# A graph-attention kernel: scores turned by transposes, or computed a second time already turned

## The reference, cut to what matters

```python
h = jnp.maximum(_layernorm(x, axis=-1), 0.0)
# layer 1: attention over the graph's neighbours
qkv = h @ W_qkv + b_qkv                       # 8 heads, 16 features each
scores = einsum('bhqd,bhkd->bhqk', q, k) / 4
attn = softmax(where(adj, scores, -inf), axis=-1)
x = x + einsum('bhqk,bhkd->bhqd', attn, v) @ W_out + b_out
h = jnp.maximum(_layernorm(x, axis=-1), 0.0)
# layer 2: causal, row-normalised similarities
A_l = zero_diag(max(cos(h @ Wl, h @ Wl), 0));  A_g = zero_diag(exp(-dist2(h @ Wg) / 2))
K = 0.9 * rows_normalised(A_l * adj) + 0.1 * rows_normalised(A_g * adj)
x = x + (K @ (h @ Wv)) @ Wo
```

## Time and profile before

| | us |
|---|---|
| median of 3 runs | 953.59 (953.18 to 954.37) |
| span of the profiled execution (first to last instruction) | 952.0 |
| PE busy | 869.2 (91%) |
| DVE busy | 800.4 (84%) |
| ACT busy | 686.6 (72%) |
| POOL busy | 189.4 (20%) |
| mean granted TensorE clock | 0.993 |

### The profile page before, as it was taken

The page is one execution under the profiler, slowest core; times in us unless marked ns, Lnnn a source line. Parts: engine busy times, 40 slices in busy tenths (PEclk is TensorE's granted clock), DMA queues, the critical chain, the costliest instruction groups (busy, mean ns, idle before and its releaser), DMA issues.

```text
span 952.0 us, 21653 instructions
## 1 busy us (share of the span) xinstructions
PE 869.2 (91%) x6067; PEld 612.4 (64%) x6067; DVE 800.4 (84%) x2460; ACT 686.6 (72%) x1185; POOL 189.4 (20%) x270
## 2 busy tenths in 40 slices
PE   2688999999999999999999999999999999999977
PEld 1454658576685857667585766758576675858565
DVE  2777889798988989898898989899898989979765
ACT  1387877787877777787777778777877878787721
POOL 1221222131212213121221312122131221211110
PEclk9899999999999999999999999999999999999999
DMA  2321212121111212111111211111121111110000
GB/s 66 94 78 51 62 34 67 57 67 33 56 55 33 66 55 66 33 55 55 36 63 55 66 36 52 55 42 59 54 66 39 50 55 51 62 35 1 12 12 12
DMA packets 62423, 47.56 MB, mean 50 GB/s; under 512 B 7600, under 2 KB 62384, under 8 KB 62384
## 3 DMA queue, kind: packets, MB, share of 16 engines
q1 hardware_dynamic: 62384, 47.09, 16.3%
HBM read 30.28 MB, written 16.78 MB: 49 GB/s over the span
## 4 chain that ended last, share of the span: by engine, by line
PE 74%; DVE 6%; issue 5%; ACT 4%; DVEq 0%; POOL 0%; ACTq 0%; POOLq 0%
PE turn L545 18%; PE pv L557 13%; PE adj L572 12%; PE adj L566 11%; PE score L535 11%; PE work L579 5%; ACT probs L919 2%; PE work L566 2%; PE work L657 2%; PE work L642 1%; DVE bn_sb L729 1%; DVE resid L861 1%; DVE masked L764 1%; ACT probs_t L912 1%; ACT col_term L964 1%
## 5 line engine op out<-in xcount | busy, mean ns | idle before, releaser
L919 ACT ACTIVATE probs<-masked,neg_max 128x512 f32<-128x512 f32 x512 | 368.6, 727 | 154.6 <-DVE neg_max L764 149.1
L764 DVE CUSTOM_DVE_ANT_0 masked<-score,mask_add 128x512 f32<-128x512 f32 x512 | 344.2, 685 | 35.3 <-PE score L535 33.8
L545 PE MATMUL turn<-ident,probs 128*128 128x128 f32 x2048 | 311.5, 274 | 3.5 <-ACT probs_t L912 2.0
L545 PEld LDWEIGHTS turn<-ident,probs 128*128 128x128 f32 x2048 | 253.4, 141 | 53.2 <-issue 9.7
L912 ACT COPY probs_t<-turn 128x512 f32<-128x512 f32 x384 | 222.4, 579 | 23.6 <-PE turn L545 23.1
L535 PE MATMUL score<-qk_rows 96*128 96x512 bf16 x512 | 198.4, 388 | 12.0 <-DVE neg_max L764 11.0
L557 PE MATMUL pv<-probs_t,v_cols 128*32 128x512 f32 x1024 | 135.7, 604 | 0.4 <-issue 0.4
L535 PEld LDWEIGHTS score<-qk_rows 96*128 96x128 bf16 x512 | 49.9, 98 | 109.5 <-DVE neg_max L764 59.1
L772 DVE COPY probs_t<-turn 128x512 f32<-128x512 f32 x128 | 87.8, 686 | 0.0
L572 PE MATMUL adj<-z,adj_cos 128*128 128x130 f32 x512 | 67.8, 276 | 1.5 <-DVE adj_cos L780 0.8
L572 PE MATMUL adj<-z,adj_rbf 128*128 128x130 f32 x512 | 67.3, 275 | 0.0
(11 more groups left out here) (101 smaller groups left out, 1025.2 us busy)
## 6 DMA issues: line engine op xcount, KB each, us to landing
qk_rows<-split_dram SPq DMA_DIRECT2D x384, 64.0 KB, 2.3
split_dram<-split SPq DMA_DIRECT2D x32, 384.0 KB, 2.6
x_sb<-in_x_dram SPq DMA_DIRECT2D x16, 256.0 KB, 2.9
out_dram<-out_sb SPq DMA_DIRECT2D x16, 256.0 KB, 2.3
masked<-in_adj_dram SPq DMA_DIRECT2D x1, 256.0 KB, 3.4
wqkv_sb<-in_L_gnn_W_qkv_dram SPq DMA_DIRECT2D x1, 192.0 KB, 2.6
bias_v<-in_L_gnn_b_qkv_dram SPq DMA_DIRECT2D x1, 64.0 KB, 3.1
bias_out<-in_L_gnn_b_out_dram SPq DMA_DIRECT2D x1, 64.0 KB, 3.8
```

Source lines behind the costliest of these rows:

```text
L545: last = pe.transpose(turn_bank[u % 2][:, j * P:(j + 1) * P], probs[:, u % 4, j * P:(j + 1) * P], ident[:, :])
L764: dve.tensor_tensor_reduce(masked[:, u % 4, :], score_bank[u % 2][:, :], mask_add[:, u % T, :], -SCALE, 3.0e38, ALU.add, ALU.min, neg_max[ ...
L919: act.activation(probs[:, u % 4, :], masked[:, u % 4, :], ACT.Exp, bias=neg_max[:, u:u + 1], scale=-1.0).then_inc(probs_ready.sem, 1)
```

## The change

What it does:

- The scaled probabilities are no longer turned. Instead each tile's scores are computed a second time with the operands changed round (k stationary, q moving), so that the keys come out on the partitions. The 96 contraction rows get three more on the q side, the negated row maxima of the queries as three bf16 parts, against rows of ones on the k side: the maxima are subtracted by the contraction.
- The mask is added to every turned tile by one more bf16 matmul into the same bank, identity times `bar_t` (0 or -2^100, turned).
- ACT takes exp straight from PSUM, with a scale and no bias, into `probs_t`. The copies by ACT and DVE (L912, L772) and the tiles `probs` and `turn_bank` are gone.
- DVE's pass over the first scores now only serves the maxima; its tile goes to `scrap`. After every 16 tiles DVE splits 16 columns of maxima into three bf16 parts (four small instructions), PE turns them, ACT copies them, and SP writes them as three contraction rows into `qk_rows` (three DMAs per half batch).
- The turned scores run 21 slots behind the scores (`LAG`) instead of 3.
- `qk_rows` is doubled, so that the next batch's rows are loaded without waiting for this batch's scores; `x_resid` has 4 buffers, `x1` 2, `v_cols` 3, and the moves by POOL (L455, L471, L483) are gone.
- The loop is gone: every engine runs over one list of slots from -32 to 583, each piece of work has a slot relative to its batch (`due`), and the pieces have new places in `AT`. The mask's setup moves ahead of the first v product; POOL's constants come first, with a memset of rows of ones in `qk_rows`.

The diff, cut to its core:

```diff
-TURN_LAG = 3
-VECTOR_UNITS = (3, 5, 6, 17, 21, 22, 27, 28)
+SLOTS = 32
+LAG = 21
 AT = {
...
+    "ln_moments": (-32,), "ln_scale": (-30,), "hT": (-29,), "hT_split": (-28,), "ln_rstd": (-27,),
+    "q": (-26,), "k": (-24,), "qk_store": (-22,), "rows0": (-18,), "x_biased": (-16,), "x_next": (-14,),
+    "v": (-12,), "rows1": (-11,),
+    "max_split": (16, 32), "max_turn": (17, 33),
+    "pv": (28, 32, 36, 40, 44, 48, 52, 56), "pv_copy": (41, 57), "y": (44, 59), "yT": (60,), "attn": (62,),
+    "ln2_moments": (63,), "ln2_rstd": (63,), "ln2_scale": (66,), "h2T": (68,), "z": (70, 71, 72, 73),
+    "z_sums": (74,), "zgT": (74,), "zgT_read": (75,), "z_norms": (76,), "col": (78,), "zlT": (79,),
+    "rbf": (81, 83, 89, 93), "rbf_exp": (82, 84, 90, 93), "rbf_mask": (84, 86, 92, 95),
+    "cos": (82, 89, 92, 94), "mix_cos": (95, 96, 100, 102), "mix_rbf": (96, 98, 100, 102), "store": (103,),
 }
+FIRST, LAST = -32, 104
...
+    def due(slot, name):
+        for nth, at in enumerate(AT[name]):
+            batch, rest = divmod(slot - at, SLOTS)
+            if rest == 0 and 0 <= batch < B:
+                return batch, nth
+        return None
...
+        qk_rows = sb("qk_rows", [P, 2, 2, H, N], BF16)
+        v_cols = sb("v_cols", [P, 3, T, H, 32])
...
SP, for s in slots:
+                if hit := due(s, "max_turn"):
+                    b, g = hit
+                    reached(sp, max_copied, b, g + 1)
...
+                    for part in range(3):
+                        sp.dma_start(
+                            qk_rows[ROWS + part:ROWS + part + 1, b % 2, 0, g * HG:(g + 1) * HG, :],
+                            max_rows[part * HALF:(part + 1) * HALF, g, :]).then_inc(max_loaded[g].sem, 16)
...
POOL, setup:
+            pool.memset(v_cols[:, :, :, :, DH + 1:32], 0.0)
+            pool.memset(v_cols[:, :, :, :, DH:DH + 1], 1.0).then_inc(s_columns.sem, 1)
+            pool.wait_ge(s_columns.sem, 1)
+            pool.memset(qk_rows[ROWS:P, :, 1, :, :], 1.0).then_inc(s_consts.sem, 1)
...
PE:
-            def turn(batch, u):
-                reached(pe, probs_ready, batch, u + 1)
...
-                for j in range(T):
-                    last = pe.transpose(turn_bank[u % 2][:, j * P:(j + 1) * P],
-                                        probs[:, u % 4, j * P:(j + 1) * P], ident[:, :])
-                last.then_inc(turned.sem, 1)
+            def turned_scores(b, w):
+                g, k = divmod(w, HALF)
+                j, hl = divmod(k, HG)
+                h = g * HG + hl
+                if k == 0:
+                    reached(pe, max_loaded[g], b)
+                reached(pe, probs_ready, b, w - 1)
+                pe.matmul(turned_bank[w % 2][:, :], ident_b[:, :], bar_t[:, j, :], start=True, stop=False)
+                pe.matmul(turned_bank[w % 2][:, :], qk_rows[0:ROWS + 3, b % 2, 1, h, j * P:(j + 1) * P],
+                          qk_rows[0:ROWS + 3, b % 2, 0, h, :], start=False,
+                          stop=True).then_inc(turned_filled.sem, 1)
...
+                if hit := due(s, "max_turn"):
+                    b, g = hit
+                    reached(pe, max_lo, b, g + 1)
+                    work_bank_free(pe, b, "max_turn", g)
+                    pe.transpose(work_bank[0:3 * HALF, 0:P // 2].bitcast(BF16),
+                                 max_parts[:, g, :, :].rearrange("p c u -> p (c u)"),
+                                 ident_b[:, :]).then_inc(max_turned.sem, 1)
...
DVE:
-                        dve.tensor_tensor_reduce(masked[:, u % 4, :], score_bank[u % 2][:, :],
-                                                 mask_add[:, u % T, :], -SCALE, 3.0e38, ALU.add, ALU.min,
-                                                 neg_max[:, u:u + 1]).then_inc(masked_ready.sem, 1)
...
-                        dve.tensor_copy(probs_t[:, h // HG, h % HG, :, t * P:(t + 1) * P],
-                                        turn_bank[u % 2][:, :].rearrange("p (j q) -> p j q", j=T)
-                                        ).then_inc(copied_vector.sem, 1)
+                    dve.tensor_tensor_reduce(scrap[:, u % 2, :], score_bank[u % 2][:, :], mask_add[:, u % T, :], -1.0,
+                                             3.0e38, ALU.add, ALU.min,
+                                             neg_max[:, u // HALF, u % HALF:u % HALF + 1]
+                                             ).then_inc(max_ready.sem, 1)
+                if hit := due(s, "max_split"):
...
+                    dve.tensor_copy(max_parts[:, g, 0, :], neg_max[:, g, :]).then_inc(max_hi.sem, 1)
+                    reached(dve, max_hi, b, g + 1)
+                    dve.tensor_tensor(max_rest[:, :], neg_max[:, g, :], max_parts[:, g, 0, :],
+                                      ALU.subtract).then_inc(max_rest_ready.sem, 1)
+                    reached(dve, max_rest_ready, b, g + 1)
+                    dve.tensor_copy(max_parts[:, g, 1, :], max_rest[:, :]).then_inc(max_mid.sem, 1)
+                    reached(dve, max_mid, b, g + 1)
+                    dve.tensor_tensor(max_parts[:, g, 2, :], max_rest[:, :], max_parts[:, g, 1, :],
+                                      ALU.subtract).then_inc(max_lo.sem, 1)
...
ACT:
-                        act.activation(probs[:, u % 4, :], masked[:, u % 4, :], ACT.Exp,
-                                       bias=neg_max[:, u:u + 1], scale=-1.0).then_inc(probs_ready.sem, 1)
...
+                if hit := tile_due(s, LAG):
+                    b, w = hit
+                    k = w // HG
+                    reached(act, turned_filled, b, w + 1)
+                    if w % HG == 0:
+                        reached(act, pv_filled, b, k - 3)
+                    act.activation(probs_t[:, k % 4, w % HG, :], turned_bank[w % 2][:, :], ACT.Exp,
+                                   scale=SCALE).then_inc(probs_ready.sem, 1)
+                if hit := due(s, "max_turn"):
+                    b, g = hit
+                    reached(act, max_turned, b, g + 1)
+                    reached(act, max_loaded[g], b - 1)
+                    act.copy(max_rows[:, g, :], work_bank[0:3 * HALF, 0:P // 2].bitcast(BF16)
+                             ).then_inc(max_copied.sem, 1)
```

More of the change, by code:

```diff
@@ L79, in graph_blocks, with tile_due @@
     HG = H // GROUPS
-    SLOTS = H * T
     ROWS = len(Q_PARTS) * DH
-    HALF = H // 2
+    HALF = SLOTS // GROUPS
+    SETS = GROUPS * T
     SCALE = float(DH) ** -0.5
     ZC = 3 * D + 2
-    assert D == P and T == 4 and HG * 32 == P
-    copied_by_vector = [u for u in range(SLOTS) if u in VECTOR_UNITS]
-    copied_by_scalar = [u for u in range(SLOTS) if u not in VECTOR_UNITS]
+    assert D == P and T == 4 and HG * 32 == P and SLOTS == H * T
+    def due(slot, name):
[4 more added lines that the diff above has]
+        return None
+    def tile_due(slot, lag):
+        batch, u = divmod(slot - lag, SLOTS)
+        return (batch, u) if 0 <= batch < B else None
+    slots = range(FIRST, LAST + SLOTS * (B - 1))
     with ExitStack() as ctx:
@@ L324, in work_bank_free @@
-        def work_bank_free(engine, i, use):
-            at = [name for name, _, _, _ in WORK_USES].index(use)
-            for back in range(1, len(WORK_USES) + 1):
-                _, sig, nth, offset = WORK_USES[(at - back) % len(WORK_USES)]
-                batch = i + offset - (1 if back > at else 0)
-                if isinstance(batch, int) and not 0 <= batch < B:
-                    continue
-                reached(engine, sig, batch, nth)
-                return
+        WORK_TURNS = sorted(
+            (AT[name][nth] + SLOTS * b, order, name, nth, b)
+            for b in range(B)
+            for order, (name, nth) in enumerate((
+                ("max_turn", 0), ("max_turn", 1), ("hT", 0), ("q", 0), ("k", 0), ("v", 0), ("y", 0), ("y", 1),
+                ("yT", 0), ("attn", 0), ("h2T", 0), ("zgT", 0), ("col", 0), ("zlT", 0))))
@@ L428, in body @@
[L428 to L445 removed]
+            pool.wait_ge(s_ident.sem, 1)
@@ L518, in rest_of_setup @@
                           stop=True).then_inc(s_wvo.sem, 1)
[L519 to L524 removed]
+                pe.wait_ge(s_ident_b.sem, 1)
                 pe.wait_ge(s_consts.sem, 1)
```

973 lines of the change are left out of this document (474 added, 499 removed).

## The result

The changed kernel takes 990.87 us (median of 4 runs, 983.95 to 998.25), the kernel before in the same comparison 953.38: ratio 1.039, 95% interval 1.034 to 1.044. It is slower by 3.9%. The forecast was 944 us, faster than before; the measured time lies above its range (918 to 962). The profiled execution took 983.95 us with a span of 981.9. The runs differ by up to 14 us among themselves; their mean granted clock was 0.989 in the fastest and 0.955 in the slowest. The kernel before has no such spread (953.0 to 954.4).

The account below looks back on a forecast made before the run. TensorE's work was taken as the bound, 55.1 us a steady period against 55.4. Span 36.5 + 33.7 + 36.5 + 46.9 + 661.2 + 49.7 + 36.0 + 42.1 = 942.6, so 944 us, range 918 to 962.

Parts of the forecast that it names:

- steps 1, 2, 3, 5: Tile stays 0.66 us; exp 0.60, ACT some 26 us a period; DVE 46.1; maxima's DMAs hidden in steady state, margin 1.4.
- rival C: Maxima's DMAs land late in every period, costing 1 us each: 956 us in all; chance 0.08.
- Rival D: Streamed bf16 matmuls cost less than 0.22 us, so DVE binds at 48 us a period: 846 us; chance 0.01.
- step 4: New order: a 10.7 us DVE chain from attn to hT's turning makes PE wait 2.7 us a period.
- the 0.71 and similar stalls go: PE's wait before pv_sb's turning vanishes, as pv sets stand every fourth slot with copy and turning 3 and 2 slots behind.
- all others at 0.7: Other hand-overs in a steady period (zlT behind col_term's copy, scores behind DVE, dispatches) cost 0.7 us together.
- The clock: Lower clock in filling: a score takes 0.44 us at 1.2 GHz, still under DVE's 0.60; costs 0 to 2 us.
- Rival A: DVE chain from attn to hT longer than counted: period 56.6 us, 963 us in all; chance 0.22.
- step 6: Fill and drain: first score at 36.5 us, first rows delayed 0 to 1.4, period 0 33.7, period 1 36.5.
- Maxima once late: First batch only: the maxima land at 25.5 us after the first score, PE wants them at 20.3, a 5.2 us stall.
- Drain: From the last score to the last attention product: 36.0 us, before 13.9, as the 21-slot lag is paid there.
- Third period: Period 2: 46.9 us, from 35.0 plus 10.4 for z, turnings, cos, rbf and one mix, stalls 1.5; before 55.4.

Follow-up runs that it names:

- b1: Kernel before the change, with exp's bias left out and ACT's copies moving half the columns: 961.41 us, stores 55.24 us apart instead of 55.40.
- e1: Changed kernel with the next batch's layer norm eight slots earlier on DVE (its root on POOL twelve): 954.95 us, ratio 1.001 to the kernel before.
- slot 22's run: Changed kernel with one extra 128x512 f32 copy on DVE per period in slot 22, outside the chain from attn to hT: 988.34 us.
- e9: e7 with POOL's residual add (x_biased) one slot later, behind its products on z_sums: 942.73 us, ratio 0.9878 to the kernel before.
- e4: e1 with the next batch's 12 row loads (rows0) three slots later, behind the maxima's DMAs: 993.85 us.
- e7: e1 with x loaded ahead of the row loads, rows0 behind the maxima's DMAs, and spare mask products in the first 21 slots: 963.34 us, ratio 1.0097.

## Why the prediction was wrong, point by point

From 944 to 990.87 us it missed by 47: some 14 in the twelve steady periods, 7 in the third period, 3 in the rest of the steady state, 12 up to tile 64, 3 in the drain, and 7 from the profiled run to the median one.

- *Bound, tile, exp, maxima (steps 1, 2, 3, 5).* Right. A tile 0.66; exp 0.598 (0.60 forecast); ACT 28.7 us a period (26 to 30), and b1 shows that it was next to never on the path of a steady period; DVE 46.4 (46.1); no DMA holds up a turned tile in a steady period, so rival C fell. Rival D fell with the tile: 0.22 us per product in the stream, not the 131 ns of the Trainium skill (TensorE: Matmul & The Clock Gate, Back-to-back issue gap); here the measurement decides.
- *The stall at hT (step 4).* Right in its place, its chain (10.15 against 10.7 us) and its sign; its size was 1.99 us by e1 where 2.7 was forecast. What failed is beside it: "the 0.71 and similar stalls go", all others at 0.7. Without hT's wait the forecast had 51.7 + 0.7 = 52.4 us; e1 measured 54.28. Of the 1.9 missing, 0.65 are waits (1.35 printed, among them the same pv_sb turning, now held by zgT_parts instead of the copy of pv) and 1.2 are TensorE's own work with its small gaps: 54.28 - 1.35 = 52.9, where the sum of products gave 51.7. The same sum gave 51.5 for before, where the period less its waits is 53.1. So the step that failed is the one that took 55.4 - 51.5 = 3.9 us for stalls to be won, when 2.3 were: TensorE's work was priced 1.2 to 1.6 us a period too low, and of the 0.7 left for the other stalls 1.35 came. Net per period 56.27 - 55.1 = 1.2 us, 14 us in twelve periods. The 1.2 us of work do not lie in one product. By the starts in one period of e1 (512.67 to 566.95), each next to its term in the sum (a turned score counted at 0.22 where the next start is printed earlier than that):

  | us | sum | e1 |
  |---|---|---|
  | tiles and pv sets | 29.8 | 30.3 |
  | cos and rbf | 5.6 | 6.2 |
  | mixes | 7.1 | 7.2 |
  | q and k | 1.4 | 1.6 |
  | v and attn | 1.8 | 1.9 |
  | turnings, z, maxima | 6.0 | 5.7 |

  The largest shares are cos and rbf, and tiles with pv. In the kernel before, whose price was taken, a three-part product takes 0.70 us behind another (530.60 to 531.30) but 0.78 behind four turns (528.45 to 529.23); the sum had 0.70 for all.
- *The clock.* The prediction took it for a matter of the filling. A wait of 1.8 to 2.1 us in the middle of dense work was followed in some periods, or in nearly all, by some three microseconds at 1.2 GHz, and each such stretch cost 1.3 to 1.65 us where it could be set against a period without one. The other runs of the changed kernel are 5 to 14 us longer than the profiled one, with a clock of 0.955 to 0.965 instead of 0.989. More slow stretches would explain it (slot 22's run has them in four periods with the same wait), but there is no trace of these runs, and e1's runs show the mean clock 0.02 apart at like times; so this is likely, not shown.
- *Rival A* gave 963 us by a longer DVE chain. The chain was shorter than it said, the period 56.3 nearly as it said (56.6), which is luck: the small waits and TensorE's own work made it up. Its time was 28 us short of the median: the filling, the drain and the clock.
- *Filling (step 6).* Up to tile 64, 106.7 us forecast and 118.4 measured. The first score came 3.1 us later: the delay of the first rows was put at 0 to 1.4, and SP issues them at 32.31 instead of 27.54. Two rows of POOL after show where from:

```profile
3.55 6.92 POOL L396 MEMSET qk_rows<- 32x8192 bf16 x1
...
27.71 2.01 POOL L422 TENSOR_TENSOR split<-resid,split 128x512 bf16<-128x512 f32 x1
```

  The memset was sized right (7, though the earlier trace rows taken per element would give 8.7), but it pushes the first root and with it the first split of q back by 3.0 us (19.75 before, 22.76 after), and the second split takes 2.01 us, not 1.15 as before. Period 0 was sized by DVE's work, 25.7 us, and the waits. DVE was busy 28.6 us of 43 and waited for scores 1 to 3 us at a time, while PE waited for DVE and for the maxima at a pace of 0.43 us a product. How the 7 us between this and e9 (32.2, below the forecast 33.7) divide among these is not separated; the spare products alone gave about 2.
- *Maxima once late.* 5.2 us forecast, 2.90 measured in the first batch and 0.82 once more; the cause was the one named, 12 row loads ahead of them on SP.
- *Drain.* 36.0 forecast, 39.1 measured, in every version with `LAG` 21. Its sum was 3 us short, and the trace after shows most of it. Behind the start of the last score stand 22 turned tiles and 8 mixes, where the sum had 21 and 7 (0.4 and 0.9 us); z to rbf with the turnings takes 12.0 us where 9.5 + 1.5 were put; the waits are 2.3 instead of 2.
- *Third period.* 46.9 forecast. It took 54.1 after (tiles 64 to 96) and 49.3 in e1 and e9, so 4.8 us of it are the x_norm wait (1.18 there) and what follows on it, the slow stretch among it, and 2.4 remain.

That e9 comes out at 942.7, next to the 944 forecast, is no merit of the sum: its periods are 0.8 us shorter than forecast because hT's wait is gone, and its ends are some 6 us longer.

## What to carry to other kernels

When a change writes a new order, list for each in-order engine what stands between a producer and its consumer, and move out what neither needs; here that was 31.8 us. Look again at both ends of every piece that is moved, its queue on SP and what runs beside it on POOL: e4 and e7 each lost more than they won by one such neighbour. Work taken from an engine that TensorE seldom waits for (ACT here, 7 us for 0.16) pays next to nothing, and a lag between two stages is paid in the drain (25 us here) whatever it saves ahead.

## What the runs showed of the hardware

- One wait of TensorE of 1.8 to 2.1 us per period of 56 us was followed by some three microseconds at 1.2 GHz (four at a mean of 0.60) in some periods and not in others. Where the longest wait was 0.84 us, and once 1.20 (e1, e9), there was none from tile 64 to the drain. The length of one wait does not settle it: in the changed kernel the clock fell at 126 us behind waits of 0.79 and 1.18 us close together.
- A DVE reduce with both inputs in SBUF takes 0.28 us alone, and 0.96 to 1.36 us beside a POOL instruction that reads SBUF, until that one ends.
- The granted clock of a window can read 1.00 where products stand 0.43 us apart (changed kernel, 37 to 73 us, two of its rows below); in e1 the same spacing stands under a clock of 0.50. The distance between starts is the surer reading.

```profile
70.20 0.63 PE L486 MATMUL score<-qk_rows 96*128 96x512 bf16 x1
70.63 0.63 PE L496 MATMUL turned<-bar_t,ident_b 128*128 128x512 bf16 x1
```
